# Mixture-of-experts stage of a one-core graph kernel: rows added to the output by accumulating scatters, final combination stage removed

## The reference, cut to what matters

```python
xf = layernorm(x1)                                  # 6250 x 256
topk_vals, topk_idx = jax.lax.top_k(xf @ Wg + bg + bias, 2)
topk_w = jax.nn.softmax(topk_vals, axis=-1)
combine = (one_hot(topk_idx, 8) * topk_w[..., None]).sum(axis=1)
h = relu(einsum('td,edh->teh', xf, W1) + b1)        # hidden size 512
y = einsum('teh,ehd->ted', h, W2) + b2
out = x1 + einsum('ted,te->td', y, combine)
```

## Time and profile before

| what | value |
|---|---|
| median of 3 runs | 2856.69 us (2856.47 to 2860.34) |
| profiled execution, its own time | 2858.14 us |
| profiled execution, span from first to last instruction | 2856.4 us |
| mean granted TensorE clock | 0.953 |
| busy share of the span: PE, DVE, ACT, POOL | 89%, 71%, 54%, 60% |

### The profile page before, as it was taken

One profiled execution on the slowest core, in us unless ns is written; L12 is line 12 of the kernel. 1 busy time (PEld: TensorE's weight loads), 2 busy tenths in 40 slices (PEclk: granted clock), 3 DMA queues, 4 the chain that ended last, 5 costly groups with the idle time before them and its releaser, 6 DMA issues. The chain is left out here.

```text
span 2856.4 us, 67306 instructions
## 1 busy us (share of the span) xinstructions
PE 2554.0 (89%) x13731; PEld 2169.2 (76%) x13732; DVE 2039.5 (71%) x5145; ACT 1549.3 (54%) x4293; POOL 1711.9 (60%) x2023
## 2 busy tenths in 40 slices
PE   1599699999999999999999999999996747999980
PEld 0244588888888888888888888888884737999980
DVE  2655788888888888888888888888886872111116
ACT  1001266666666666666666666666664224666650
POOL 3000377777777777777777777777775213555540
PEclk9999899999999999999999999999998559999995
DMA  6132577677777767777777767777762532222218
GB/s 212 36 110 105 178 215 207 207 210 212 207 210 207 206 204 207 207 209 214 208 207 208 207 204 210 209 211 211 206 202 73 158 114 61 71 70 70 70 61 270
DMA packets 304076, 490.12 MB, mean 172 GB/s; under 512 B 52058, under 2 KB 217692, under 8 KB 303580
## 3 DMA queue, kind: packets, MB, share of 16 engines
q0 software_dynamic: 81152, 259.63, 31.7%
q1 hardware_dynamic: 215548, 214.12, 23.6%
q10 hardware_dynamic: 7056, 12.85, 1.4%
HBM read 435.86 MB, written 51.41 MB: 171 GB/s over the span
## 5 line engine op out<-in xcount | busy, mean ns | idle before, releaser
L744 POOL DMA_INDIRECT kv_ring<-vk_table,idx_c x880 | 880.0, 1000 | 654.4 <-issue 242.7
L881 PE MATMUL ps_e<-we_sb,aT 128*128 128x256 f32 x3520 | 910.2, 381 | 11.0 <-DVE kqq L971 9.4
L965 DVE TENSOR_TENSOR ve_ke<-kv_ring,ps_e 128x512 f32<-128x512 f32 x880 | 603.4, 686 | 181.7 <-PE ps_e L884 111.2
L881 PEld LDWEIGHTS ps_e<-we_sb,aT 128*128 128x128 f32 x3520 | 602.3, 191 | 58.6 <-issue 9.0
L815 ACT COPY aT<-ps_t 128x256 f32<-128x256 f32 x880 | 326.8, 371 | 468.8 <-PE ps_t L869 334.9
L754 POOL TENSOR_TENSOR w_ring<-ve_ke,ea 128x264 f32<-128x264 f32 x880 | 562.7, 640 | 30.3 <-PE ps_u L934 10.0
L934 PE MATMUL ps_u<-w_ring,sel 128*128 128x264 f32 x1760 | 548.6, 394 | 6.6 <-DVE acc L1031 3.7
L884 PE MATMUL ps_e<-q_sb,selT 128*128 x1760 | 524.6, 380 | 0.0
L1031 DVE TENSOR_TENSOR acc<-acc,ps_u 128x264 f32 x880 | 370.0, 420 | 24.8 <-DVE acc L1019 11.7
L954 DVE TENSOR_REDUCE alpha<-kqq 128x8 f32<-128x256 f32 x880 | 367.9, 418 | 7.2 <-issue 5.2
L884 PEld LDWEIGHTS ps_e<-q_sb,selT 128*128 128x128 f32 x1760 | 335.4, 191 | 46.0
(11 more groups left out here) (250 smaller groups left out, 2669.0 us busy)
## 6 DMA issues: line engine op xcount, KB each, us to landing
a_ring<-in_edge_attr SPq DMA_DIRECT2D x880, 128.0 KB
loc_c<-loc_table SPq DMA_DIRECT2D x55, 512.0 KB
kv_ring<-vk_table,idx_c POOLq DMA_INDIRECT x880
vk_table<-kv_out SPq DMA_DIRECT2D x49, 256.0 KB, 2.0
got<-y_table ACTq DMA_DIRECT2D x49, 256.0 KB, 3.8
skip_table<-skip_out SPq DMA_DIRECT2D x49, 128.0 KB, 1.7
skip<-skip_table SPq DMA_DIRECT2D x7, 896.0 KB, 7.1
xn_table<-acc SPq DMA_DIRECT2D x7, 896.0 KB, 4.9
```

What stands on the lines that cost most here:

```text
L744: g.indirect_dma_start(out=kv_ring[:, i % N_KV, :], out_offset=None, in_=vk_table, in_offset=bass.IndirectOffsetOnAxis(ap=idx_c[:, par, i: ...
L881: t.matmul(ps_e[i % 2][:, 0:D], aT[i % 2][:, k * P:(k + 1) * P], we_sb[:, k, :], start=(k == 0), stop=(k == KD - 1))
L965: v.tensor_tensor(both, kv.rearrange("p (t h c) -> p t h c", t=2, c=C), by_head(e, C)[:, None, :, :].to_broadcast([P, 2, H, C]), ALU.add). ...
```

## The change

The combination moves into the expert loop. In stage c4 SP also stores `x1` to `out`, after the weight loads, in two DMAs (48 tiles, then 106 rows). A row of `xn_table` becomes 258 long: 256 values and the node's two gates (the first, and the second minus the first), stored by a DMA of SP in c5. `take` therefore brings the gates beside the rows, DVE picks the slot's gate, adds `b2`, multiplies by the gate, and `put` adds the 128 rows to `out` in HBM with an accumulating scatter, dropping slots beyond the last node. Two blocks can hold the same node, so each scatter waits until the one before has landed. Stage c8 is gone.

```diff
-        xn_table = dram("xn_table", (NR, D))
-        y_table = dram("y_table", (NR * TOP + NB * P, D))
+        xn_table = dram("xn_table", (NR, D + TOP))
...
@@ stage c4, sync @@
-                    sp.dma_start(xn_table[j * P:(j + n) * P, :].rearrange("(j p) d -> p j d", p=P),
+                    sp.dma_start(xn_table[j * P:(j + n) * P, 0:D].rearrange("(j p) d -> p j d", p=P),
                                  xn2[:, j:j + n, 0:D]).then_inc(xn_stored, 16)
...
+                sp.wait_ge(x1_ready, NGR)
+                sp.dma_start(out[0:(NT - 1) * P, :].rearrange("(j p) d -> p j d", p=P), x1[:, 0:NT - 1, :]).then_inc(x1_stored, 16)
+                sp.dma_start(out[(NT - 1) * P:N, :], x1[0:NTAIL, NT - 1, :]).then_inc(x1_stored, 16)
                 sp.wait_ge(xn_stored, 16 * NGR)
@@ stage c5, gpsimd and vector @@
-                nc.gpsimd.iota(spare_i[:, :], [[P, NB]], base=TOP * NR + 1, channel_multiplier=1).then_inc(bi_set, 1)
...
-                v.tensor_copy(spare[:, :], spare_i[:, :])
...
+                v.tensor_copy(gates[:, :, 0], gate_w[:, 0, :]).then_inc(gates_ready, 1)
+                v.tensor_tensor(gates[:, :, 1], gate_w[:, 1, :], gate_w[:, 0, :], ALU.subtract).then_inc(gates_ready, 1)
...
-                then(v.scalar_tensor_tensor(out=unused[:, :], in0=held[:, :], scalar=0.0, in1=spare[:, :], op0=ALU.is_equal, op1=ALU.mult))
-                v.tensor_scalar(take_i[:, :], held1[:, :], 1, None, ALU.logical_shift_right)
-                v.scalar_tensor_tensor(out=put_i[:, :], in0=unused[:, :], scalar=-1.0, in1=held[:, :], op0=ALU.add, op1=ALU.add)
+                then(v.tensor_scalar(unused[:, :], held[:, :], 0.0, float(PAD_DST), ALU.is_equal, ALU.mult))
+                v.tensor_scalar(second_i[:, :], held1[:, :], 1, None, ALU.bitwise_and)
+                then(v.tensor_scalar(take_i[:, :], held1[:, :], 1, None, ALU.logical_shift_right))
+                v.tensor_copy(second[:, :], second_i[:, :])
+                then(v.tensor_copy(taker[:, :], take_i[:, :]))
+                v.tensor_tensor(put_i[:, :], taker[:, :], unused[:, :], ALU.add)
+
+            @block.sync
+            def _(sp):
+                sp.wait_ge(gates_ready, 2)
+                with nc.allow_non_contiguous_dma(reason="two gates beside each token's row"):
+                    sp.dma_start(xn_table[:, D:D + TOP].rearrange("(j p) k -> p j k", p=P), gates[:, :, :]).then_inc(gates_stored, 16)
+                sp.wait_ge(gates_stored, 16)
@@ stage c7, gpsimd @@
                 def take(b):
                     pool.wait_ge(s["x_turned"], at("x_turned", b - 2))
+                    pool.wait_ge(s["gate_read"], at("gate_read", b - 2))
...
                 def put(b):
                     pool.wait_ge(s["y_ready"], at("y_ready", b))
+                    if b:
+                        pool.wait_ge(y_stored[(b - 1) % 2], 16 * ((b - 1) // 2 + 1))
+                    else:
+                        pool.wait_ge(x1_stored, 16 * 2)
                     nc.gpsimd.indirect_dma_start(
-                        out=y_table, out_offset=bass.IndirectOffsetOnAxis(ap=put_i[:, b:b + 1], axis=0),
-                        in_=y[b % 2][:, :], in_offset=None).then_inc(y_stored[b % 2], 16)
+                        out=out, out_offset=bass.IndirectOffsetOnAxis(ap=put_i[:, b:b + 1], axis=0),
+                        in_=y[b % 2][:, :], in_offset=None, bounds_check=N - 1, oob_is_err=False,
+                        compute_op=ALU.add).then_inc(y_stored[b % 2], 16)
@@ stage c7, tensor @@
-                    pe.wait_ge(s["y_ready"], at("y_ready", b - 2))
+                    pe.wait_ge(s["y_biased"], at("y_biased", b - 2))
@@ stage c7, vector @@
+                def read_gate(b):
+                    dve.wait_ge(x_loaded[b % 2], 16 * (b // 2 + 1))
+                    v.scalar_tensor_tensor(out=gate_of[:, b:b + 1], in0=t_in[b % 2][:, D + 1:D + 2], scalar=second[:, b:b + 1],
+                                           in1=t_in[b % 2][:, D:D + 1], op0=ALU.mult, op1=ALU.add).then_inc(s["gate_read"], 1)
+
+                def weigh(b, ex):
+                    dve.wait_ge(s["y_summed"], at("y_summed", b))
+                    v.tensor_tensor(y_full[b % 2][:, :], ps_y[b % 2][:, 0:D], b2_sb[:, bass.ds(ex * D, D)],
+                                    ALU.add).then_inc(s["y_biased"], 1)
+                    dve.wait_ge(s["y_biased"], at("y_biased", b))
+                    dve.wait_ge(s["gate_read"], at("gate_read", b))
+                    if b >= 2:
+                        dve.wait_ge(y_stored[b % 2], 16 * (b // 2))
+                    v.tensor_scalar(y[b % 2][:, :], y_full[b % 2][:, :], gate_of[:, b:b + 1], None, ALU.mult).then_inc(s["y_ready"], 1)
+
+                for b in range(NB + 2):
+                    ex = expert_of(dve, b - 2) if b >= 2 else None
+                    if b < NB:
+                        read_gate(b)
+                    if b >= 2:
+                        weigh(b - 2, ex)
...
-        with ExitStack() as c8:
```

More of the change, by code:

```diff
@@ L125, in gnn_ffn @@
         chunk_tile = sb("chunk_tile", [P, NCH])
-        assert NT * NE <= IT and TOP * NT <= IT and NB <= IT
+        assert NT * (NE + TOP) <= IT and TOP * NT + NB <= IT and TOP == 2
         assert 2 * NB <= IT
@@ L130, in gnn_ffn @@
         put_i = src_idx[:, NB:2 * NB]
+        second = dst_loc[:, TOP * NT:TOP * NT + NB]
         gate_w = dst_loc[:, 0:TOP * NT].rearrange("p (k j) -> p k j", k=TOP)
         logits = mask[:, 0:NT * NE].rearrange("p (j e) -> p j e", e=NE)
+        gates = mask[:, NT * NE:NT * (NE + TOP)].rearrange("p (j k) -> p j k", k=TOP)
         block_expert = item_row[0:1, 0:NB]
@@ L1066, in gnn_ffn @@
         experts_loaded = sem("experts_loaded")
+        x1_stored = sem("x1_stored")
         with ExitStack() as c4:
@@ L1282, in gnn_ffn @@
             nb = sb5("nb", [P, NB])
-            spare_i = sb5("spare_i", [P, NB], I32)
             held1 = sb5("held1", [P, NB], I32)
+            second_i = sb5("second_i", [P, NB], I32)
             rest = flat(acc[:, :, :])[:, TOP * NT * P:(NT + 1) * UW]
-            spare, held, unused = [rest[:, i * NB:(i + 1) * NB] for i in range(3)]
+            held, taker, unused = [rest[:, i * NB:(i + 1) * NB] for i in range(3)]
             NQ = 7
@@ L1306, in gnn_ffn @@
             hi_used = sem("hi_used", c5)
+            gates_ready = sem("gates_ready", c5)
+            gates_stored = sem("gates_stored", c5)
             block = c5.enter_context(nc.Block())
@@ L1373, in _ @@
                     then(v.tensor_tensor(rank[:, :, :], rank[:, :, :], more[:, :, :], ALU.add))
-                dve.wait_ge(bi_set, 2 + TOP)
+                dve.wait_ge(bi_set, 1 + TOP)
                 v.tensor_copy(nb[:, :], nb_i[:, :])
-                v.tensor_copy(spare[:, :], spare_i[:, :])
                 v.tensor_copy(holder[:, :], holder_i[:, :])
@@ L1448, in gnn_ffn @@
                       for i in range(2)]
-            t_in = [sb7(f"t_in{i}", [P, D]) for i in range(2)]
+            t_in = [sb7(f"t_in{i}", [P, D + TOP]) for i in range(2)]
+            gate_of = sb7("gate_of", [P, NB])
             tT = [sb7(f"tT{i}", [P, D]) for i in range(2)]
             hT = [sb7(f"hT{i}", [P, F]) for i in range(2)]
+            y_full = [sb7(f"y_full{i}", [P, D]) for i in range(2)]
             y = [sb7(f"y{i}", [P, D]) for i in range(2)]
@@ L1456, in gnn_ffn @@
             s, at, grant = counters(c7, loaded=0, x_turned=2, tT_ready=2, h_summed=2, w1_ready=0, hT_ready=2,
-                                    y_summed=3, y_ready=2, act_pace=0, dve_pace=0)
+                                    y_summed=3, y_biased=2, y_ready=0, gate_read=2, act_pace=0, dve_pace=0)
             x_loaded = [sem(f"x_loaded{i}", c7) for i in range(2)]
@@ L1598, in _ @@
                 v = nc.vector
-                grant(dve, "y_ready")
+                grant(dve, "y_biased", "gate_read")
                 dve.wait_ge(s["loaded"], 16 * 2)
[L1601 to L1610, removed]
@@ L1612, in _ @@
-                over_blocks(dve, emit)
-        with ExitStack() as c8:
[L1618 to L1657, removed]
```

## The result

The changed kernel takes 2911.58 us (median of 4 runs, 2909.28 to 2912.88); the kernel before takes 2858.49 on the same occasions. The ratio is 1.0185 with a 95% interval of 1.0167 to 1.0203: 1.9% slower. The prediction was 2816 us and faster; its range ended at 2884.

The account below looks back on a forecast made before the run. PE was taken to bound the expert loop at 3.73 us a block, with c8 an uncovered memory pass. -67.4 + 22 + 0.5 + 1.0 + 2.5 = -41.4 us gave 2816 us; range 2803 to 2884.

Parts of the forecast that it names:

- put(b): Expert loop c7: each scatter waits for the previous landing; period max(3.73, L + 0.28) us, so the wait is hidden.
- L: Time of a put in c7 from start of issue to landing; taken as 3.0 us, free up to 3.45.
- hand-over: In c7, from release of POOL's wait to the start of the put's issue; taken as 0.28 us.
- only the transport doubles: Middle estimate for an accumulating put in c7: one issue, doubled transport, 0.99 + 1.4 + 1.4 = 3.8 us.
- the put chain as the period: Rival in c7: POOL's wait before each put sets the period; 2958 us with L = 4.8; chance 0.24.
- c8 taken out: End of the program: the final combination, a memory pass that nothing covers, disappears; -67.4 us.
- x1 stored in c4: End of c4: two more DMAs hold SP's queue and lengthen the stage; +22 us, bounds 1 and 26.
- Stores of xn_table at the odd pitch: In c4: rows of 1032 bytes might slow the stores; +0.5 us, bounds 0 and 5.
- c5: Stage c5: DVE's added small steps cost +1.0 us; the gates' store, 6.4 us, is covered by 56 us of work.
- take(b) and DVE's new steps: In c7: gather starts some 0.9 us later, DVE goes from 0.42 to about 1.2 us a block; free.
- The last puts and the drain: End of c7: the last put lands 2.5 us later; POOL's drain of 8.2 us keeps its length.

Follow-up runs that it names:

- e2: Changed kernel with plain scatters in place of accumulating ones, wait and bounds check kept, addition to x1 left out; 2815.49 us in one run.
- e1: Changed kernel with scatters adding into an internal table with spare rows, no bounds check, table copied to the output at the end; 2926.8 us, ratio 1.0233.
- e5: e1 with x1 stored in c5 and a put's two waits swapped, so the landing wait stands in the scatter's own instruction; 2863.11 us, ratio 1.0009.
- e4: Changed kernel with the two x1 stores issued at the start of c5 instead of the end of c4; 2891.46 us, ratio 1.0109.
- e3: e4 with odd blocks adding into a side table, each put waiting for the put two blocks before, final sum left out; 2794.34 us in one run.
- v1: Changed kernel with slots sorted by choice, then expert, puts waiting two blocks back and once at the middle, x1 stored in c5; 2825.54 us, ratio 0.9875.
- e6: Changed kernel with only the order of a put's two waits swapped, register move still ahead of the scatter; 2908.58 us in one run.

## Why the prediction was wrong

**The step that failed** is the one on put(b): "the period becomes max(3.73, L + 0.28)", with "so I take L = 3.0". Two of its terms were too small. L measured 3.8 us in the median, and the hand-over 0.88. Together they make 4.7 us, and from the first put to the last 4.65 were measured, 0.92 over PE's period; 105 x 0.92 = 97 us, which is nearly all of c7's 98.6.

*L.* I took the value nearest to a plain scatter (2.4), and no row priced the addition. The addition costs on both sides: POOL's issue 1.58 us in place of 0.99, and 2.2 us from its end to the landing in place of 1.4. e2 shows that both come from the addition, e1 that the bounds check has almost no part in it. The value for "only the transport doubles" in the text was 3.8, nearly right as a sum but for another reason: the transport did not double, and the issue grew, which I had held fixed. The Trainium skill (DMA: Bandwidth & Descriptors, Two DMAs through the same engine are not ordered) reports a read-modify-write packet that read before the one ahead of it had written, and I took from it that L would stay under 3.8. The trace does not bear it out: the median stands at that bound, 3.8, and the longest put took 4.2. Whether the rows of one engine overlap no run here shows.

*The hand-over.* 0.28 us was read where the awaited value stood in the scatter's own wait. The changed kernel waits for two things and sets a register, so the landing is awaited ahead. By the rule with 0.28, L = 3.8 would have given a period of 4.08 and 2853 us, 0.2% under the kernel before; with L = 3.0 and a hand-over of 0.88 it would have been 3.88 and 2832. By these two estimates neither term alone makes the kernel slower, and both together do. e5, with the short hand-over, has a period of 4.13 and equals the kernel before, with 20 us less for its store of x1 and 22.4 us more for its final copy.

*The rival on the other side*, the put chain as the period, was this mechanism, with the right place and the price too low by those 0.6 us a block. Its threshold, L = 3.85 us, was therefore wrong; with a hand-over of 0.88 it is near 3.2.

**The other steps held.**

- *c8 taken out*, -67.4: e2, where the put chain is hidden, takes 2815.5 us, close to the 2816 forecast for a hidden chain. That it is so close is in part luck: c4 and c5 grew by 20.8 us and not by 23.5, and the stages ahead of c4, which the change leaves alone, took 1.3 us longer in that run. c7 grew by 2.6 (2.5 forecast). The sum as written also ends at 2815.3 (2816.7 - 1.45) and not at 2816.
- *x1 stored in c4*: +22 forecast, +19.8 measured. The long issue was 16.85 us, against the 18.15 that I scaled from, and the one before it 2.92 against 3.3; together they are the 19.8, so the 0.5 us added beside them stood for nothing. e4 confirms it as a cause: 20 us come back.
- *Stores of xn_table at the odd pitch*: they landed in 5.8 us in place of 4.9, but c4's arithmetic was as long as before (from DVE's first step in it to its last 90.3 us both times; behind that DVE waited for SP). Nothing, where I took 0.5.
- *c5*: +0.8 for +1.0. The gates' store landed in 9.1 us in place of the 6.4 scaled from the load: a little dearer, and far inside its cover of 56 us. The Trainium skill (DMA: Bandwidth & Descriptors, Specifications) has a read-modify-write for transfers below 512 B, which points that way; no run here shows it as the cause.

```profile
L1450 SPq DMA_DIRECT2D xn_table<-mask x1: 391/391/391, 2336.1 to 2336.1; - x1
...
DMA to landing us min/median/max: 9.1/9.1/9.1
```

- *take(b) and DVE's new steps*: hidden, as e3 shows (DVE had 107 us of work in its c7 of 416.6, and POOL idled 0.85 us a block).
- *The last puts and the drain*: the drain was not the 8.2 us that I kept, but 6.5.

```profile
L1456 POOLq COMPARE_BRANCH  x1: 46/46/46, 2900.6 to 2900.6; - x1
L1456 POOLq DRAIN  x1: 6467/6467/6467, 2900.8 to 2900.8; - x1
```

## What to carry to other kernels

When a wait for a transfer is put between two transfers of one queue, the period of that chain is issue + time from its end to the landing + hand-over. Price all three, and ask how much each may grow before the chain passes the bound. Here PE's 3.73 us left 1.05 us over the plain scatter's 2.4 with a hand-over of 0.28, and 0.45 with one of 0.88; the addition alone took 1.4. A price for an operation that no row shows should be bounded by the issue as well as by the transport. And rather than shorten such a chain, look for an order of the work in which the wait isn't needed: sorting by choice left c5 and c7 together 31 us longer than in the kernel before, where the chain had made them 99 us longer.

## What the runs showed of the hardware beyond that

- Accumulating scatters of 128 rows of 1 KB went with packets between 512 B and 2 KB, about one a row, plain ones with none of that size and with packets over 2 KB (the changed kernel and e2); POOL issued one in 1.58 us in place of 1.02.
- A wait in an instruction of its own ahead of POOL's scatter cost about 0.45 us a block more than the same wait in the scatter (e1 to e5, 4.56 to 4.13), but if it has already passed, the scatter starts 0.30 us behind the gather, as in the kernel before (e3). Why was not tried.
- Two accumulating scatters in flight, into one tensor but with no row in common, did not slow the loop: v1's period is PE's 3.73 us.
- POOL's drain at the end of c7 took 8.23 us with plain scatters (before and e2), 6.47 in the changed kernel, e1 and e3 to e6, where they accumulate, and 3.28 in v1, where they accumulate too; its row stands below. What sets it stays open.

```profile
L1460 POOLq DRAIN  x1: 3282/3282/3282, 2819.2 to 2819.2; - x1
```
